# TensorE multiplies the identity while it waits for normalisations, and layer 3's row scores rotate over three PSUM banks

## What is computed

```python
x = x + _L0_xattn_ref(ctx_1024, _layernorm(x), L0_xattn_Wq)   # 56 queries, first 56 context rows as keys
x = x + _L0_ffn_ref(_layernorm(x), ...)       # 8 experts, the best two weighted
x = x + _L1_xattn_ref(_layernorm(x), ctx_1024, ...)  # self attention, cross attention, two dense layers
x = x + _L1_ffn_ref(_layernorm(x), ...)       # quantised
x = x + _L2_xattn_ref(_layernorm(x), ctx_1024, ...)  # 16 heads of 64 over 1500 keys
x = x + _L2_ffn_ref(_layernorm(x), ...)
x = x + _L3_xattn_ref(_layernorm(x), ctx_1024, mask_BxS2_bk0, ...)  # 16 heads of 8 over 1500 keys
x = x + _L3_ffn_ref(_layernorm(x), ...)       # 8 experts, each output normalised
```

## Time and profile before

| | |
|---|---|
| Runs | 1691.65, 1690.0, 1689.13 us; median 1690.0 |
| The profiled execution's own time | 1691.79 us |
| Its span, first to last instruction | 1690.1 us |
| Mean granted TensorE clock, share of 2.4 GHz | 0.936 |
| Busy: PE, PEld, DVE, ACT, POOL | 87%, 73%, 77%, 51%, 21% |
| Stages touched by bursts, us from the span's start | l0a 9 to 40, l0f 41 to 150, l1s 152 to 201, l1c 201 to 314, l2fold 382 to 413 |
| Layer 3's attention | 1109 to 1541 |

### The profile page before, as it was taken

One profiled execution on the slowest core, in us unless ns is written; L12 is line 12 of the kernel. 1 busy time (PEld: TensorE's weight loads), 2 busy tenths in 40 slices (PEclk: granted clock), 3 DMA queues, 4 the chain that ended last, 5 costly groups with the idle time before them and its releaser, 6 DMA issues. The chain is left out here.

```text
span 1690.1 us, 38992 instructions
## 1 busy us (share of the span) xinstructions
PE 1471.1 (87%) x14907; PEld 1233.3 (73%) x14907; DVE 1299.8 (77%) x2618; ACT 866.9 (51%) x1330; POOL 347.8 (21%) x462
## 2 busy tenths in 40 slices
PE   3796396647999999999999999869999999996995
PEld 2685264346899999999999998437777777774995
DVE  4776664685888888888888886657888888884688
ACT  1474132324666666666666664335666656652332
POOL 0230000002333333333333330030111110100320
PEclk8798698757999999999999999979999999998998
DMA  1387084101111111111111100045456455531010
GB/s 39 109 222 184 4 217 111 37 0 32 43 37 38 37 36 36 37 56 43 45 37 36 36 0 5 2 125 125 111 123 146 113 128 134 120 87 52 26 38 23
DMA packets 94193, 119.67 MB, mean 71 GB/s; under 512 B 12288, under 2 KB 78385, under 8 KB 94073
## 3 DMA queue, kind: packets, MB, share of 16 engines
q1 hardware_dynamic: 94072, 117.95, 27.3%
HBM read 80.09 MB, written 0.49 MB: 48 GB/s over the span
## 5 line engine op out<-in xcount | busy, mean ns | idle before, releaser
L1899 ACT CAST l2att_PT<-PS 125x512 fp32r<-125x512 f32 x336 | 175.3, 595 | 221.3 <-PE PS L1838 221.3
L2633 DVE TENSOR_REDUCE l3att_parts<-PS 112x1 f32<-112x500 f32 x384 | 245.6, 668 | 54.0 <-PE PS L2371 47.1
L1939 DVE TENSOR_REDUCE l2att_neg<-PS 128x1 f32<-128x1500 f32 x112 | 192.7, 1720 | 78.0 <-PE PS L1831 78.0
L1945 DVE TENSOR_TENSOR l2att_PT<-PS,l2att_PT 125x512 fp32r<-125x512 f32 x336 | 210.0, 680 | 1.5 <-ACT l2att_PT L1899 1.5
L2500 ACT ACTIVATE l3att_P<-PS 125x1344 f32<-125x1344 f32 x128 | 165.2, 1291 | 78.1 <-PE PS L2392 78.1
L1838 PEld LDWEIGHTS PS<-all_ident,l_P 128*125 128x125 f32 x1344 | 163.6, 187 | 14.0 <-DVE l_P L1953 5.3
L1908 ACT ACTIVATE l_P<-PS,l2att_neg 128x1500 f32<-128x1500 f32 x112 | 171.0, 1527 | 4.5 <-DVE l2att_neg L1939 4.5
L1870 PE MATMUL PS<-l2att_PT,l_cc 125*128 125x256 f32 x576 | 170.5, 296 | 0.0
L1838 PE MATMUL PS<-all_ident,l_P 128*125 128x128 f32 x1344 | 165.4, 273 | 3.9 <-DVE l_P L1953 3.9
L1872 PE MATMUL PS<-l2att_PT,l_cc 125*128 125x256 f32 x576 | 162.5, 282 | 0.0
L1874 PE MATMUL PS<-l2att_PT,l_cc 125*128 125x256 f32 x576 | 162.3, 282 | 0.0
(11 more groups left out here) (563 smaller groups left out, 2959.2 us busy)
## 6 DMA issues: line engine op xcount, KB each, us to landing
l3att_KS<-l3att_kh SPq DMA_DIRECT2D x128, 187.5 KB, 4.1
l_cT<-in_ctxT SPq DMA_DIRECT2D x18, 750.0 KB, 7.4
l_c<-in_ctx SPq DMA_DIRECT2D x16, 750.0 KB
l3att_cT<-in_ctxT SPq DMA_DIRECT2D x16, 750.0 KB, 4.4
l3att_KS<-l3att_kl SPq DMA_DIRECT2D x64, 187.5 KB, 4.2
l_QP<-in_ctx SPq DMA_DIRECT2D x10, 672.0 KB
l_QP<-in_ctxT SPq DMA_DIRECT2D x8, 750.0 KB, 6.7
l0f_w<-in_L_ffn_W SPq DMA_DIRECT2D x16, 256.0 KB, 3.1
```

Of the source, the lines that this page charges most:

```text
L1899: act.copy(PT[:, 4 * g:4 * g + 4, PLACE[u1], 0, :], PS[0:CHUNK, 3 * s1 + g, :].rearrange("k (c r) -> k c r", r=128)).then_inc(hi_in, 1)
L1939: v.tensor_reduce(neg[:, s:s + 1], E, XY_AXES, ALU.max, negate=True).then_inc(top_in, 1)
L1945: v.tensor_tensor(PT[:, 4 * g:4 * g + 4, at, 1, :], PS[0:CHUNK, 3 * s1 + g, :].rearrange("k (c r) -> k c r", r=128), PT[:, 4 * g:4 * g + 4 ...
L2633: v.tensor_reduce(parts[:, u % 2, half, i:i + 1], PS[0:HROWS, PLACES[p], 0:BANK_KEYS], X_AXIS, ALU.max, negate=True).then_inc(top_in, 1)
```

## The change

A helper issues float32 products of the identity with itself into a PSUM bank that nothing holds at that time. Twelve calls of it are put into TensorE's queues, 338 products in all. In `attend_sets` the row scores go to banks 0, 2 and 7 in turn, bank 1 is left to keys and denominators, outputs and transposed maxima both go to bank 6, the third row product comes ahead of the key projection, and VectorE takes the second maximum after the copy of the transposed maxima instead of before it. The waits follow the new banks.

```diff
+    def keep_busy(self, pe, bank, count):
+
+        for _ in range(count):
+            pe.matmul(self.PS[:, bank, 0:128], self.ident[:, :], self.ident[:, :], start=True, stop=True)
...
 local_attention, TensorE
+                self.keep_busy(pe, 6, 30 if self_keys else 5)
                 pe.wait_ge(w_in, 80 if self_keys else 32)
                 pe.matmul(PS[:, 7, 0:128], ...).then_inc(fold_ps, 1)
+                if not self_keys:
+                    self.keep_busy(pe, 6, 14)
                 for k in range(2):
                     pe.wait_ge(xn_ready, k + 1)
...
                 if self_keys:
+                    self.keep_busy(pe, 7, 14)
                     pe.wait_ge(cnt_in, 1)
...
+                self.keep_busy(pe, 7, 52 if self_keys else 30)
                 pe.wait_ge(p_done, 1)
...
                     mm.then_inc(z_ps, 1)
+                if self_keys:
+                    self.keep_busy(pe, 7, 44)
...
 first_experts, TensorE
                 pe.wait_ge(w_in, 64)
+                self.keep_busy(pe, 6, 28)
                 for k in range(2):
                     pe.wait_ge(xn_ready, k + 1)
...
+                self.keep_busy(pe, 6, 5)
                 pe.wait_ge(xt_in, 2)
...
 cross_attention, TensorE
                     mm.then_inc(z_ps, 1)
+                self.keep_busy(pe, 0, 40)
                 pe.wait_ge(n2_ready, 1)
...
                     mm.then_inc(y_ps, 1)
+                self.keep_busy(pe, 2, 46)
...
 project_heads, TensorE
+                self.keep_busy(pe, 0, 30)
                 for k in range(2):
                     pe.wait_ge(xn_ready, k + 1)
...
 attend_sets
-        PLACES = (0, 2, 0, 2, 0, 1)
+        PLACES = (0, 2, 7, 0, 2, 7)
+        OUT = 6
...
                                 if known != 0:
-                                    pe.wait_ge(top_in, 6 * n - 1)
-                            elif 2 <= p <= 4:
-                                pe.wait_ge(top_in, 6 * n + p - 1)
-                            elif p == 5:
-                                if known is None or known >= 1:
-                                    pe.wait_ge(top_in, 6 * n)
-                                if g < BANKS and more:
-                                    pe.wait_ge(kl_in, b * BANKS + BANKS + g + 1)
-                                if weighs:
-                                    pe.wait_ge(den_in, n // SETS)
+                                    pe.wait_ge(top_in, 6 * n - 2)
+                            elif n > 0 or p >= 3:
+                                pe.wait_ge(top_in, 6 * n + p - 2)
+                            elif p == 2:
+                                pe.wait_ge(blank, 1)
...
+                    if now:
+                        rows((2,))
                     if g < BANKS and more:
                         if g == 0:
                             pe.wait_ge(ct_in[1 - u // SETS], (b + 1) // 2 * 16 + 16)
+                            if n >= UNROLL:
+                                pe.wait_ge(den_in, (n - 1) // SETS)
+                        else:
+                            pe.wait_ge(kl_in, b * BANKS + BANKS + g)
                         project_keys(pe, 1 - u // SETS, g, SIDE)
...
-                    if now:
-                        rows((2,))
...
 attend_sets, VectorE
                     if now:
-                        tops((0, 1))
+                        tops((0,))
...                  the copy of the transposed maxima
                     if now:
-                        tops((2,))
+                        tops((1, 2))
```

More of the change, by code:

```diff
@@ L2399, in maxima @@
                             pe.wait_ge(o_in, n - 2)
+                        if known == 1:
+                            pe.wait_ge(blank, 1)
                         pe.wait_ge(negs_in, n)
                         for half in range(2):
-                            mm = pe.transpose(PS[0:3, 6 + (u - 1) % 2, 256 + HROWS * half:256 + HROWS * half + HROWS],
+                            mm = pe.transpose(PS[0:3, OUT, 256 + HROWS * half:256 + HROWS * half + HROWS],
                                               negs[:, (u - 1) % 2, half, :].bitcast(F32), ident[0:HROWS, 0:HROWS])
@@ L2407, in values @@
                         s, a = (u - 2) % UNROLL // SETS, (u - 2) % SETS
-                        pe.wait_ge(m_in, n - 1)
+                        pe.wait_ge(m_in, min(n, GROUPS))
                         if known is None or known >= 4:
@@ L2412, in values @@
                         pe.wait_ge(p_in, 2 * n - 2)
-                        if known == 2:
-                            pe.wait_ge(blank, 1)
                         for k in range(CHUNKS):
                             for h in range(SETS):
-                                mm = pe.matmul(PS[QUAD * h:QUAD * h + VCOLS, 6 + u % 2, 0:TOK],
+                                mm = pe.matmul(PS[QUAD * h:QUAD * h + VCOLS, OUT, 0:TOK],
                                                VS[s][:, k, a, h, :], P[u % 2][:, k, TOK * h:TOK * h + TOK],
@@ L2432, in one @@
                         pe.wait_ge(o_in, n - 3)
+                        if more:
+                            pe.wait_ge(kl_in, b * BANKS + 2 * BANKS)
+                        elif n > 2 * UNROLL:
+                            pe.wait_ge(den_in, n // SETS - 1)
                         pe.matmul(PS[:, SIDE, 0:SET_ROWS], SEL[:, :, :].rearrange("p h c -> p (h c)"),
@@ L2507, in outputs @@
                         act.wait_ge(o_ps, n - 1)
-                        act.copy(OC[:, bass.ds((n - 2) // SETS, 1), a, :], PS[:, 6 + u % 2, 0:TOK].unsqueeze(1)
+                        act.copy(OC[:, bass.ds((n - 2) // SETS, 1), a, :], PS[:, OUT, 0:TOK].unsqueeze(1)
                                  ).then_inc(o_in, 1)
@@ L2622, in _ @@
                 v.wait_ge(t2_in, 2 * SETS)
-                v.memset(PS[:, 6:8, 0:TOK], 0.0).then_inc(blank, 1)
+                v.memset(PS[:, OUT, 0:TOK], 0.0).then_inc(blank, 1)
                 def one(n, u, known):
@@ L2641, in one @@
                         v.tensor_copy(QB[a // SETS][96:99, a % SETS, :],
-                                      PS[0:3, 6 + a % 2, 256:256 + SET_ROWS]).then_inc(m_in, 1)
+                                      PS[0:3, OUT, 256:256 + SET_ROWS]).then_inc(m_in, 1)
                     if now:
-                        tops((2,))
+                        tops((1, 2))
                     if g < BANKS and (known is None or known < GROUPS - SETS):
```

## The result

| | before | with the change |
|---|---|---|
| Runs of this comparison, median us | 1692.18 (20 runs, 19 of them 1689.1 to 1695.3) | 1682.78 (20 runs, 19 of them 1677.0 to 1689.9) |
| Ratio, 95% interval | | 0.9944 [0.9931, 0.9957] |
| The profiled execution, us | 1691.79 | 1677.03 |
| Mean granted clock in it | 0.936 | 0.965 |

One run of 20 in each column, 2497 and 2182 us, is far longer than the rest and counts in the median, but not in the ratio, its interval or the ranges. The change makes the kernel faster by 9.5 us, 7.3 to 11.7 by the interval. The profiled execution is among the fastest of the change's, 14.8 us under the one of before. Those 19 runs lie 12.8 us apart with the change and 6.1 before: that spread needs an explanation too.

The account below looks back on a forecast made before the run. It took the kernel as bound in layers 0 and 1 by TensorE products at half clock after idle waits, in layer 3 by nearly full TensorE and VectorE. Gains of 11.3 outside layer 3 plus 1.6 there, 12.9, gave 1677 us, range 1669 to 1685.

Parts of the forecast that it names:

- The price of a product: TensorE, every burst: one identity product takes 0.43 us at the low clock and 0.22 at the high one.
- l0a, 0.9 and 2.6: Layer 0's attention: bursts of 5 and 14 products ahead of XN gain 0.9 us, a later one of 30 gains 2.6.
- l0f, 0.3, late by 1.5: Layer 0's experts: 28 products end likeliest 1.5 us late, yet gain 0.3 us, bounds -2 and +1.5.
- l1s front, 0.8: Start of layer 1's self attention: 30 products gain likeliest 0.8 us, bounds -0.5 and 2.3.
- l1s tail, 1.75: Later in layer 1's self attention: 14 and 52 products in one pause let the chain behind run high, gaining 1.75 us.
- l1c front, 1.6, and end, 2.5: Layer 1's cross attention: 44 products ahead of its weight product gain 1.6 us, 40 ahead of its dense layers 2.5.
- 46 products, nothing: Layer 1's cross attention: 46 products in a 12.35 us wait gain nothing, as what follows is ahead of its consumers.
- l2fold, 0.8: Start of the head projection: 30 products end late but gain likeliest 0.8 us, bounds -0.4 and 2.0.
- Rival 1: Tight bursts of 28, 30 and 30 in l0f, l1s and l2fold overrun their waits: 1683 us, chance 0.15.
- Layer 3, 1.6: Layer 3's attention loop: the low keys' wait goes, VectorE then limits; 0.1 us per four steps, 16 times, bounds 0 and 7.5.
- rival 2: Layer 3 gives all of the low keys' wait because VectorE does not hold the transposes: 5.9 us more, 1671, chance 0.12.
- The clock's phase: Timing of low-clock stretches: a us or two allowed at the range's ends, around 1671 and 1683.

Follow-up runs that it names:

- second measurement: The change itself, unaltered, measured once more against the kernel before: 1681.07 us, ratio 0.9939.
- the three shorter bursts: The change with 20 instead of 28 products in layer 0's experts, 22 instead of 30 in layer 1's self attention, 16 instead of 30 in head projection: 1674.48 us.
- layer 3 alone: The kernel before with only the change's `attend_sets`, no identity products anywhere: 1690.24 us, ratio 0.9996.
- the bursts alone: The change's twelve bursts with layer 3's attention as in the kernel before: 1686.83 us, ratio 0.9974, 4.4 us faster.

## Why the prediction was right, and where it was not

The time measured, 1682.78, lies in the range (1669 to 1685), 5.8 above the forecast of 1677; on the shown median of 1690.0 the ratio gives 1680.5. The gain was forecast at 13 and is 9.5 (7.3 to 11.7), in the second measurement 10.3. The profiled execution's 14.8 is luck: it is the fastest of 19.

- **The price of a product**, 0.22 high and 0.43 low: 52 in 11.86 us, 80 in 18.03, and 0.44 low. An overrun costs its whole length (7.1 us for 40 products too many, of which 1.7 us fell into the wait). Shown, by one trace each.
- **l0a, 0.9 and 2.6.** From the transposes to VectorE's last sum 7.80 us before, 5.25 now: 2.55. With the stage's 3.8, 1.3 for the front.
- **l0f, 0.3, late by 1.5.** The low stretch of 4.2 us was in the burst, as worked out. XN was whole at 48.80 and the transposes began at 50.27: 1.5 late. The stage gained 0.8 in this trace, 0.5 in the mean of seven, and 2.1 with 20 products.
- **l1s front, 0.8.** From weight product to the softmax's transposes 24.30 us before, 22.42 now, and 0.25 later after the stage's start: 1.6. The loss set against it, a clock that is down at the burst's start, did not come in this trace (0.50 nowhere in it); it did in that of the three shorter bursts.
- **l1s tail, 1.75.** 17.93 before, 16.22 now: 1.7.
- **l1c front, 1.6, and end, 2.5.** Weight product to first scores 5.59 and 4.29: 1.3. From the transposes to the next stage 19.77 and 17.63: 2.1.
- **46 products, nothing:** 0.2, within what this stage differs by between traces (66.7 to 68.5).
- **l2fold, 0.8:** -0.4 in the change's trace, the bad end of its bounds, and -0.1 in the mean of seven. Rival 1 was right about this burst and that of l0f: shorter ones gave 2.9 us back. The head projection's burst ended 8.56 us after the stage's start, which is the branch that the prediction gives for a fallen clock (390.5 from 381.9); what it had wrong is the weight, since its likeliest value leans on the other branch, and the clock was low at this burst's start in the trace.
- **Layer 3, 1.6.** The mechanism was right in each part: the wait for the low keys went, one for `l3att_negs` came, and the 7.5 of rival 2 did not. The term was mis-sized: "I take 0.1 a step of four, 16 times" measured about 0.02, against which 0.7 stand for the one round whose first step has no reciprocal. About 1 us in all. That the two traces differ by 1.7 there is partly chance: the first round took 26.84 before and 24.39 now, but 24.28 and 24.40 in two other traces with the old banks, and the change's third and fourth rounds were 1.9 longer than most. This attention took 431.6 to 435.8 us in seven traces with the new banks and whole reciprocals and 434.2 to 438.1 in three with the old ones.
- **What was missing:** the loop of cross attention was taken to cost the same whatever happens around it. In eight traces with the same code there the stage took 105.7 to 112.2 us, by where the clock's low stretches fell on the first and last pair and by the wait for one load (the table above); before the change it took 113.6 and, in the run with layer 3 alone, 112.6. So the stage's gain is 0.4 to 7.9 us. The forecast had 4.1. Of the 6.6 of the profiled execution the bursts made 3.4, as said, and 3.0 came from the load and the last pair, which stood at 1.6 and 2.8 in the trace of before, on the scale of the table, and at 0.1 and 1.2 in this one: luck of the draw.
- **The clock's phase** was put at "a us or two". Executions of the same kernel lie 12.8 us apart, and their mean clocks go with it: 0.964 to 0.969 in those under 1680 us, 0.958 to 0.960 in those over 1688 (in the second measurement one of 1688.1 had 0.962). The table above places 6.5 us of such a spread in one stage, 2.2 of them a load and not the clock; that the rest is the clock's too is argued, not shown.

The parts, with the means of the traces where several have the same code (two without bursts, seven or more with): l0a 3.9, l0f 0.5, l1s 3.1, cross attention's two bursts 3.4, head projection -0.1, layer 3 about 1. That is 11.8 where the sum had 12.9: l0a, l1s and l0f came out 1.1 higher, cross attention, the head projection and layer 3 2.2 lower. The medians say 9.5 and 10.3. The 1.5 to 2.3 us between lie about within their intervals, and no run places them; nor do these parts agree with the 4.4 of the bursts alone. It would take traces of several executions of one kernel.

## What to carry to other kernels

Work that only keeps TensorE's clock up is to be sized so that it ends ahead of the wait even if its first part runs at the lower clock: here 16 products brought the clock up as 30 did in the trace shown, and the stage was 1.2 us shorter in the mean. Where a wait goes and the next one stands at the same moment, look for what fills the engine that is now late, and move that into the step where it has slack: the 0.84 us reciprocal one step later made the freed bank worth 0.6 us in each of 13 rounds, where it had been worth 0.02. Once the clock's low stretches or a load decide, one profiled execution is one draw, so compare stages over several traces before a difference is put down to a change.

## What the runs showed of the hardware that was not expected

- Float32 transposes of the identity bring the clock up as products do (0.50 from 371.7 to 375.1 in the head projection's burst and 1.00 behind; windows at 0.98 to 1.00; ratio 0.9963 against 0.9944 and 0.9939, intervals overlapping).
- After the same pause of 1.98 us in cross attention's loop the clock was low at different places in traces of the same code (203.1 to 206.5, over work that is hidden, or, behind a further pause of 2.40, 208.1 to 214.9, over work that is not), and executions of one program lay 12.8 us apart.
- One stage's wait for one load was 0 in one trace and 1.89 and 2.23 us in others of the same code there. The cause was not tried.
- The third and fourth round of layer 3 took 0.5 to 1.7 us more than 25.0 each in three traces and nothing more in the others: in the change's trace TensorE stood there for 1.3 us in three places which the profile marks as "issue". The cause was not tried.
